# A mixture of experts behind two normalizations: rounds reordered, epsilons on GpSimd, rows on ScalarE, and experts of the slots found by partition

## The reference, cut to what matters

```python
h = (x - mu) * rsqrt(var + 1e-05) * ln_g + ln_b          # over the features of a token
h_norm = (h - m_t) * rsqrt(v_t + 1e-08)                  # over the tokens of a sequence, by feature
gamma, beta = ...                                        # a small network over the sequence's subject
h = h_norm * (softplus(gamma) + 1e-08) + beta
probs = softmax(h @ router_w)                            # 8 experts
gates, idx = top_k(probs, 2)                             # normalized to a sum of 1
y = sum over the two of gate * (relu(h @ w1[e] + b1[e]) @ w2[e] + b2[e])
x = x + y
...                                                      # gradients of x on a grid, one explicit step, max with 0
```

## Time and profile before

| what | value |
|---|---|
| median of 3 runs | 361.11 us (361.04 to 361.63) |
| profiled execution | 361.7 us, its span 359.9 us |
| TensorE busy | 306.2 us (85%) |
| VectorE busy | 291.9 us (81%) |
| ScalarE busy | 251.2 us (70%) |
| GpSimd busy | 156.8 us (44%) |
| rounds and routing | up to 72.9 us of the span |

### The profile page before, as it was taken

One profiled execution on the slowest core, in us unless ns is written; L12 is line 12 of the kernel. 1 busy time (PEld: TensorE's weight loads), 2 busy tenths in 40 slices (PEclk: granted clock), 3 DMA queues, 4 the chain that ended last, 5 costly groups with the idle time before them and its releaser, 6 DMA issues.

```text
span 359.9 us, 6561 instructions
## 1 busy us (share of the span) xinstructions
PE 306.2 (85%) x1961; PEld 265.4 (74%) x1961; DVE 291.9 (81%) x540; ACT 251.2 (70%) x462; POOL 156.8 (44%) x122
## 2 busy tenths in 40 slices
PE   1758312899999999999999999999999988379896
PEld 1548211889999999999999999999999978133334
DVE  4998892778899889988988989888898893289991
ACT  1668104596998799699789969969987870278421
POOL 1344424133335545533534554453354413277650
PEclk9999755799999999999999999999999999769999
DMA  7912508985688877866868786686784500595822
GB/s 248 387 35 73 162 1 291 358 270 207 220 263 264 292 241 224 272 226 215 283 231 274 263 277 195 240 258 214 227 277 157 157 4 29 158 308 111 184 96 82
DMA packets 49860, 74.46 MB, mean 207 GB/s; under 512 B 3349, under 2 KB 40623, under 8 KB 49712
## 3 DMA queue, kind: packets, MB, share of 16 engines
q1 hardware_dynamic: 45104, 62.29, 52.8%
q0 software_dynamic: 4368, 11.54, 10.6%
q10 hardware_dynamic: 368, 0.39, 0.4%
HBM read 63.69 MB, written 9.31 MB: 203 GB/s over the span
## 4 chain that ended last, share of the span: by engine, by line
PE 66%; DVE 15%; DMA 8%; issue 5%; POOL 2%; ACT 1%; SPq 1%; DVEq 0%; POOLq 0%; ACTq 0%
PE psum L991 23%; PE psum L1018 19%; PE psum L1020 10%; PE psum L984 5%; PE psum L960 2%; DMA x_sb<-in_x_dram 2%; PE psum L986 2%; DMA t_y<-y_rows 2%; PE psum L1013 2%; DMA raw_b<-in_L_cond_exp_w_dram 2%; DVE st L1149 1%; PE psum L1055 1%; DMA x_sb<-t_y 1%; DVE z L1139 1%; DVE h_tok L1175 1%
## 5 line engine op out<-in xcount | busy, mean ns | idle before, releaser
L787 POOL DMA_INDIRECT gathered<-h_rows,src_cur x40 | 62.1, 1554 | 119.6 <-DVE src_cur L1321 105.7
L1018 PE MATMUL psum<-w_split,hid 128*128 128x512 f32 x296 | 107.2, 404 | 1.5 <-DVE y_sb L1373 1.5
L991 PE MATMUL psum<-slot_h,w_split 128*128 128x256 f32 x768 | 96.5, 286 | 2.5 <-DVE slot_h L1338 2.5
L991 PEld LDWEIGHTS psum<-slot_h,w_split 128*128 128x128 f32 x768 | 94.6, 193 | 3.6 <-issue 3.0
L1020 PE MATMUL psum<-w_split,hid 128*128 128x256 f32 x296 | 83.1, 281 | 0.0
L1332 DVE TENSOR_TENSOR w_split<-raw_b,w_split 128x2048 fp32r<-128x2048 f32 x23 | 52.7, 2292 | 22.3 <-ACT w_split L605 22.3
L1018 PEld LDWEIGHTS psum<-w_split,hid 128*128 128x128 f32 x296 | 55.6, 188 | 14.4 <-issue 1.7
L637 ACT ACTIVATE hid<-relu 128x512 fp32r<-128x512 f32 (+1 forms) x92 | 51.1, 592 | 16.0 <-DVE relu L1344 16.0
L800 POOL DMA_INDIRECT y_rows<-y_sb,dst_cur x39 | 48.7, 1249 | 28.8 <-issue 11.6
L628 ACT ACTIVATE relu<-psum,b_cur 128x256 f32<-128x256 f32 x128 | 53.7, 490 | 6.2 <-PE psum L991 4.1
L1326 DVE TENSOR_TENSOR w_split<-raw_a,w_split 128x2048 fp32r<-128x2048 f32 x23 | 52.6, 2286 | 6.0 <-DMA gathered<-h_rows,src_cur 5.0
(11 more groups left out here) (181 smaller groups left out, 403.9 us busy)
## 6 DMA issues: line engine op xcount, KB each, us to landing
raw_a<-in_L_cond_exp_w_dram SPq DMA_DIRECT2D x23, 1024.0 KB, 6.0
raw_b<-in_L_cond_exp_w_dram SPq DMA_DIRECT2D x23, 1024.0 KB, 5.7
t_y<-y_rows SPq DMA_DIRECT2D x6, 512.0 KB, 8.7
x_sb<-in_x_dram SPq DMA_DIRECT2D x4, 512.0 KB, 7.9
h_rows<-h_tok SPq DMA_DIRECT2D x16, 128.0 KB, 2.2
x_sb<-t_y POOLq DMA_DIRECT2D x4, 512.0 KB, 4.7
out_dram<-t_out SPq DMA_DIRECT2D x3, 512.0 KB, 3.0
b_all<-in_L_cond_exp_b_dram SPq DMA_DIRECT2D x1, 1024.0 KB, 10.9
```

Source lines behind the costliest of these rows:

```text
L787: pool.indirect_dma_start(out=gathered[:, par, t, :], out_offset=None, in_=h_rows, in_offset=bass.IndirectOffsetOnAxis(ap=src_cur[:, par, ...
L991: last = pe.matmul(banks[bank][:, ST * (blk % 2):ST * (blk % 2) + rows], w_split[:, 0, par, w, at:at + P], slot_h[:, par, h, k, 0:rows], s ...
L1018: pe.matmul(out.rearrange("p (w d) -> p w d", w=2), hid[:, par, 0, blk, P * t:P * t + P], w_split[:, 1, par, :, D * blk:D * blk + D], star ...
```

## The change

- The two additions of epsilon (`var1`, `var2`) move from VectorE to GpSimd, ahead of each power.
- A round on VectorE is written in another order: both kinds of statistics, then `z`, then (rounds 9 to 11) the copy `rows` of sequences 1 to 3, then `aff_a`, the aggregations, `aff_m` and `aff_b`. Semaphores of their own replace `link`.
- ScalarE makes the copies `rows` of sequences 0, 6 and 7; VectorE keeps 1 to 5.
- TensorE runs `forward(6)` ahead of `back(0)`, and `back(1)` behind `forward(7)`.
- The experts of the slots are found with a slot on each of 23 partitions, on VectorE: two comparisons and a sum over the experts. TensorE turns the column of 23 into a row, and VectorE copies it to `e_idx` behind `pick`. GpSimd's three operations go, and 366 columns of constants with them. `gathered_part` is only padding that keeps the addresses.
- `low_w1(0)` waits for `first_sent`, which GpSimd raises behind the two gathers of slot 0, and not for their landing.

Declarations of semaphores are left out of the diff.

```diff
@@ -88,8 +88,8 @@
     c[:, C_BEFORE:C_BEFORE + P] = p[:, None] < p[None, :]
     c[:, C_LATER:C_LATER + NJ * E] = np.tile(np.arange(E) > 0, NJ)
     lead = np.array([first_col(s) for s in range(NS)])
-    c[:, C_SLOT:C_SLOT + NS * E] = np.repeat(lead // TB, E)
-    c[:, C_SLOT + NS * E:C_SLOT + 2 * NS * E] = np.repeat(np.where(lead < ROWS, E, NC - 1 - lead), E)
+    c[0:NS, C_SLOT] = lead // TB
+    c[0:NS, C_SLOT + 1] = np.where(lead < ROWS, E, NC - 1 - lead)
     c[:, C_PART] = p
     c[:, C_PART + 1] = p + 1
     d1, d2 = stencil(T)
@@ -263,8 +263,9 @@
             row_of = own("row_of", [P, P, TOPK * NJ], F16)
             col_of = own("col_of", [P, NC, TOPK * NJ], F16)
             token_of = own("token_of", [P, TOPK * NJ], F16)
-            e_cmp = own("e_cmp", [1, 2, NS, E])
-            e_sum = own("e_sum", [1, NS])
+            e_cmp = own("e_cmp", [NS, 2, E])
+            e_sum = own("e_sum", [NS, 1])
+            own("gathered_part", [P, 2 * NS * E + NS - 2 * E - 1])
             second = own("second", [P, NC])
             empty = own("empty", [P, NC])
             token = own("token", [P, NC])
@@ -397,10 +401,11 @@
         STYLE = 5
         CHUNK = 8
         HELD = 6
+        BY_SCALAR = (0, NB - 2, NB - 1)
 
         def rows_taken(b):
 
-            return (htok_ok, b + 1)
+            return (htok_act, BY_SCALAR.index(b) + 1) if b in BY_SCALAR else (htok_ok, b)
 
         def rows_bank(b):
             return (6, 2, 0)[b % 3]
@@ -562,6 +567,13 @@
                                           bias=aff_b[:, b, k:k + 1], scale=aff_a[:, b, k:k + 1])
                 last.then_inc(ht_ok, 1)
 
+            def rows(b):
+
+                at = rows_bank(b)
+                act.wait_ge(back_t, b + 1)
+                act.activation(h_tok[:, 2 * b:2 * b + 2, 0:KD * P + E], psum[:, at:at + 2, 0:KD * P + E],
+                               ACT.Copy).then_inc(htok_act, 1)
+
             act.wait_ge(sty_in, 32)
             front(0)
             for n in range(STYLE - 1):
@@ -583,9 +595,13 @@
             styled(1)
             front(6)
             styled(2)
+            rows(0)
             front(7)
             for b in range(3, NB):
                 styled(b)
+
+            for b in BY_SCALAR[1:]:
+                rows(b)
 
             act.wait_ge(gap_ok, 1)
             act.activation(e2[:, :], gap[:, :], ACT.Exp).then_inc(e2_ok, 1)
@@ -754,10 +770,16 @@
             for i in range(NB + 3):
                 if i < NB:
                     pool.wait_ge(var1_ok, i + 1)
+                    pool.tensor_scalar(var1[:, 2 * i:2 * i + 2], mv1[:, 2 * i:2 * i + 2, 1], 1e-5, None,
+                                       ALU.add).then_inc(eps1_ok, 1)
+                    pool.wait_ge(eps1_ok, i + 1)
                     pool.tensor_tensor(rs1[:, 2 * i:2 * i + 2], var1[:, 2 * i:2 * i + 2], half[:, 0:2],
                                        ALU.pow).then_inc(rs1_ok, 1)
                 if i >= 3:
                     pool.wait_ge(var2_ok, i - 2)
+                    pool.tensor_scalar(var2[:, i - 3, :], mv2[:, i - 3, :, 1], 1e-8, None,
+                                       ALU.add).then_inc(eps2_ok, 1)
+                    pool.wait_ge(eps2_ok, i - 2)
                     pool.tensor_tensor(rs2[:, i - 3, :], var2[:, i - 3, :], half[:, 0:KD],
                                        ALU.pow).then_inc(rs2_ok, 1)
             for c in range(TOPK):
@@ -765,17 +787,6 @@
                 number(token_of[:, NJ * c:NJ * c + NJ], [[sign * P, NJ]], base=sign, by_partition=sign)
             number(col_of[:, :, :], [[1, NC], [0, TOPK * NJ]])
             number(row_of[:, :, :], [[1, P], [0, TOPK * NJ]])
-
-            pool.wait_ge(off_ok, 1)
-            pool.tensor_tensor(e_cmp[:, :, :, :],
-                               cst[0:1, C_SLOT:C_SLOT + 2 * NS * E].rearrange("p (c s e) -> p c s e", c=2, e=E),
-                               t_off[0:1, :, :].rearrange("p c (a e) -> p c a e", a=1).broadcast_to([1, 2, NS, E]),
-                               ALU.subtract).then_inc(e_link, 1)
-            pool.wait_ge(e_link, 1)
-            flags = e_cmp[:, :, :, :].rearrange("p c s e -> p (c s e)")
-            pool.tensor_scalar(flags, flags, 0.0, None, ALU.is_ge).then_inc(e_link, 1)
-            pool.wait_ge(e_link, 2)
-            pool.tensor_tensor(e_cmp[:, 0, :, :], e_cmp[:, 0, :, :], e_cmp[:, 1, :, :], ALU.mult).then_inc(e_link, 1)
 
             def gather(k, m):
                 s, par = at_slot(k, m), k % 2
@@ -805,6 +816,8 @@
             pool.wait_ge(hrows_out, 16 * (NJ + 1))
             for k in range(FIRST):
                 gather(k, None)
+                if k == 0:
+                    pool.sem_inc(first_sent, 1)
             for k in range(2, FIRST):
                 gather(k + 2, None)
                 scatter(k - 2, None)
@@ -922,12 +935,11 @@
             forward(3)
             forward(4)
             forward(5)
+            forward(6)
             pe.wait_ge(eye_ok, 1)
             back(0)
-            forward(6)
-            back(1)
             forward(7)
-            for b in range(2, NB):
+            for b in range(1, NB):
                 back(b)
 
             pe.wait_ge(m_ok, 1)
@@ -939,6 +951,8 @@
                                  m_bf[:, 0:NJ + 1 - d, :].rearrange("p j e -> p (j e)"), start=False, stop=(d == NJ))
             last.then_inc(rank_ok, 1)
 
+            pe.wait_ge(e_sum_ok, 1)
+            pe.matmul(banks[4][0:1, 0:NS], e_sum[:, :], ident[0:NS, 0:NS], start=True, stop=True).then_inc(e_turned, 1)
 
             pe.wait_ge(tok_ok, 1)
             for t in range(TOPK * NJ):
@@ -1130,6 +1144,12 @@
                         dve.wait_ge(x_in[i // 2], 16)
                     for j in range(2 * i, 2 * i + 2):
                         last = dve.bn_stats(st1[:, j, :], x_sb[:, j, :])
+                if do_chan:
+                    dve.wait_ge(pre_ok, chan + 1)
+                    for k in range(KD):
+                        last = dve.bn_stats(st2[:, chan, k, :], h_pre[:, k, T * chan:T * chan + T])
+                if do_tok or do_chan:
+                    chained(last)
                 b = i - 1
                 if tokens and 0 <= b < NB:
                     dve.wait_ge(rs1_ok, b + 1)
@@ -1139,32 +1159,26 @@
                         norm = dve.tensor_scalar(z[:, j % 4, :], x_sb[:, j, :], mv1[:, j, 0:1], rs1[:, j:j + 1],
                                                  ALU.subtract, ALU.mult)
                     norm.then_inc(z_ok, 1)
+                if i - NB in range(1, NB):
+                    rows(i - NB)
                 if do_aff:
                     dve.wait_ge(rs2_ok, b1)
-                    last = dve.tensor_tensor(aff_a[:, b0:b1, :], rs2[:, b0:b1, :],
-                                             gam[:, :, b0:b1].rearrange("p k b -> p b k"), ALU.mult)
-                if do_chan:
-                    dve.wait_ge(pre_ok, chan + 1)
-                    for k in range(KD):
-                        last = dve.bn_stats(st2[:, chan, k, :], h_pre[:, k, T * chan:T * chan + T])
-                if not (do_tok or do_aff or do_chan):
-                    return
-                link(last)
+                    dve.tensor_tensor(aff_a[:, b0:b1, :], rs2[:, b0:b1, :],
+                                      gam[:, :, b0:b1].rearrange("p k b -> p b k"), ALU.mult).then_inc(aff_a_ok, b1 - b0)
+                dve.wait_ge(chain, steps[0])
                 if do_tok:
                     for j in range(2 * i, 2 * i + 2):
                         last = dve.bn_aggr(mv1[:, j, :], st1[:, j, :])
-                if do_aff:
-                    last = dve.tensor_tensor(aff_m[:, b0:b1, :], mv2[:, b0:b1, :, 0], aff_a[:, b0:b1, :], ALU.mult)
+                    last.then_inc(var1_ok, 1)
                 if do_chan:
                     for k in range(KD):
                         last = dve.bn_aggr(mv2[:, chan, k, :], st2[:, chan, k, :])
-                link(last)
-                if do_tok:
-                    dve.tensor_scalar(var1[:, 2 * i:2 * i + 2], mv1[:, 2 * i:2 * i + 2, 1], 1e-5, None,
-                                      ALU.add).then_inc(var1_ok, 1)
-                if do_chan:
-                    dve.tensor_scalar(var2[:, chan, :], mv2[:, chan, :, 1], 1e-8, None, ALU.add).then_inc(var2_ok, 1)
+                    last.then_inc(var2_ok, 1)
                 if do_aff:
+                    dve.wait_ge(aff_a_ok, b1)
+                    dve.tensor_tensor(aff_m[:, b0:b1, :], mv2[:, b0:b1, :, 0], aff_a[:, b0:b1, :],
+                                      ALU.mult).then_inc(aff_m_ok, b1 - b0)
+                    dve.wait_ge(aff_m_ok, b1)
                     dve.tensor_tensor(aff_b[:, b0:b1, :], sty[:, KD:2 * KD, b0:b1].rearrange("p k b -> p b k"),
                                       aff_m[:, b0:b1, :], ALU.subtract).then_inc(aff_ok, b1 - b0)
 
@@ -1172,8 +1186,8 @@
 
                 dve.wait_ge(back_t, b + 1)
                 at = rows_bank(b)
```

(23 more changed lines are left out.)

11 lines of the change are left out of this document (7 added, 4 removed).

## The result

The changed kernel took 358.56 us (median of 5 runs, 356.84 to 359.56), the kernel before 361.04 on the same chip (360.43 to 361.63): a ratio of 0.9922, 95% interval 0.9897 to 0.9948. The profiled execution took 359.56 us with a span of 357.7.

What follows compares the result with a forecast made beforehand. The chain ending last was taken to bound it: normalization rounds, routing, first gather, w2 load, then matmuls. 0.55 + 1.14 - 1.05 = 0.64 won gave 361.06 profiled, 360.5 as median; range 358.7 to 361.8 us.

Steps and rivals of the forecast that it cites:

- the rounds: Normalization rounds up to the first maximum mx: mx at 38.4 instead of 38.95, 0.55 us won.
- the stretch behind the first gather: W2 load (5.68 us), its split, then matmuls from 72.90: taken as unchanged, passing earlier gains on in full.
- Routing, 1.14 forecast: Finding the experts, from t_off on: 1.14 us won, or 0.2 if the slow VectorE instructions have another cause.
- First gather, 1.05 lost: Slot 0's second gather meets the early w1 subtraction and lands at 62.55 instead of 61.5: 1.05 us lost.
- the equal gaps of 0.30: Equal 0.30 us gaps between gather starts, read as GpSimd's sequencer running ahead, so first_sent rises before the second gather.
- The rival in which the gather isn't met: first_sent rises late or w1 is split after 58.2; the gather wins 0.5, time 358.9; chance 0.29.
- The rise of TensorE's rate: Doubling of TensorE's pass rate, placed near 30.0 during back(1); front 1.0 won if at 29, 0.3 if at 32.
- e: Price of one epsilon addition on GpSimd, taken as 0.40 us, between a memset (0.11) and a power (0.69).
- The rival of a better front: e near 0.16 or TensorE's rate doubled by 29: front wins 1.1, time 359.9 with the gather met; chance 0.12.
- From there on the chain is matmuls behind matmuls: From 72.90, the slots' matmuls: an earlier microsecond won counts in full at the end.
- swallowed by round 4: Smaller constants may bring x_sb sooner, but round 4's wait for h_pre of sequence 1 takes that gain up.
- Dear epsilons, the slower rival: Additions on GpSimd cost 1.16 us like its only tensor_scalar, rounds become GpSimd's, time 367; chance 0.14.

Runs made afterwards that it cites:

- the parts alone: Two kernels, each the kernel before with one half of the change: the new rounds, 359.23 us; the new way to find the experts, 358.60 us.
- the landing awaited: The changed kernel with low_w1(0) waiting again for the landing of slot 0's gather: 357.13 us, ratio 0.9890.
- epsilons twice: The changed kernel with each epsilon added on GpSimd as two halves, one behind the other: 360.07 us (one run).
- the nine and the six matmuls: Unread matmuls behind forward(5), low_w1(0) awaiting the landing: nine, 357.13 us; six, with the copies rows(1) to rows(3) behind the affine factors, 355.79 us.

## Why the prediction was wrong, point by point

Two steps failed: the rounds, whose term of 0.55 measured 1.57, and the stretch behind the first gather, taken over unchanged, where the w2 load took 0.56 more and the slots 0.75 less. The routing and the first gather came out as summed.

**Routing, 1.14 forecast: right.** 1.11 in the result, 1.12 between the parts alone. `base` fell from 0.85 to 0.15 when GpSimd's operations went, as the prediction read it; an instruction of VectorE was also put ahead of it, so that cause isn't shown by itself. TensorE's turn of the 23 values, put at some 0.6 from no row, took 0.23 and was hidden.

**First gather, 1.05 lost: right in mechanism and nearly in size, incomplete in reach.** The gather was met, as the equal gaps of 0.30 had it; 0.94 lost to the landing. The step that failed is the load behind it, taken over at 5.68: the w2 load took 6.24, since it started among the rows of slot 1's gathers, whose generation ended 0.68 us past its issue (60.44 against 59.76). In the kernel before it ended 0.13 past it:

```profile
60.69 0.94 POOL L787 DMA_INDIRECT gathered<-h_rows,src_cur  x1 [0.30 <-issue]
```

Together 1.5. The load of w1 for slot 2 isn't the cause, though it goes out sooner: 1.79 us into the w2 load here, 2.56 before, but 2.57 again with the landing awaited, where the w2 load still takes 6.13. The rival in which the gather isn't met was given 0.5 won by a faster landing. With the landing awaited that gain is there (2.75 for 3.32) and the w2 load takes it back (6.13 for 5.68).

**Rounds, 0.55 forecast: the term that failed, by its size.** The order of events was right to the names. The rise of TensorE's rate, placed near 30.0 from one trace, came at 30.0 in the profiled execution; that was luck, since it came at 27.0 with the same program in another, worth 1.35 of `mx`. So at the forecast's own place of the rise the term measured 1.57, 1.02 more than forecast. Of that 0.68 was won when `rows(1)` started, at 29.82 instead of 30.5, since z of sequence 6 stood at 23.42 instead of 24.2; the other 0.34 lies between `rows(1)` and `mx`, 7.56 where 7.9 was summed. What was mis-sized is above all e: it was 0.22, not the 0.40 midway between a memset and a power. By "epsilons twice", where 0.30 of e moves z by 0.98, the 0.18 too much make some 0.6 at z (an estimate), and they count once more, 0.18, in the last addition ahead of `mx`. The other quarter of a microsecond is the rest of the sum, priced a little long. How steeply `mx` depends on e was right: by the prediction's figures for 0.10, 0.40 and 0.69 an e of 0.52 costs 0.8 more than one of 0.22, and at an equal rise it cost some 0.9. The rival of a better front (doubling by 29, or e near 0.16) came nearest, at 1.1.

**"From there on the chain is matmuls behind matmuls", counted in full: not so.** The matmuls of the slots themselves became 0.75 faster, because narrower constants moved the tiles. The prediction read the 366 columns as a shorter load alone, and that part (swallowed by round 4) was right.

**Dear epsilons, the slower rival: fell.** The trace's only `tensor_scalar`, 1.16 on 368 elements, was no guide to two elements. The Trainium skill, GPSIMD Engine Reference, section Engine selection, wants elementwise work on VectorE, but puts its price on operations of two inputs and calls those of one input roughly line-rate, and the addition of an epsilon has one. The traces here have the addition at 0.22 to 0.26 us on GpSimd and 0.15 to 0.17 on VectorE, and moving it back to VectorE won nothing.

In the terms of the sum: 0.55 + 1.14 - 1.05 = 0.64 became 1.57 + 1.11 - 0.94 - 0.56 + 0.75 = 1.93, and 0.22 in the tail. The tail varied from 49.3 to 50.5 between executions, so that 0.22 can't be put down to the change. That the medians differ by 2.48 and the profiled executions by 2.14 lies within what the rise of TensorE's rate alone moves.

**Open.** What makes TensorE's rate rise 3.0 us apart in two executions whose work up to it agrees within 0.05 isn't settled; earlier work moves it, as the nine and the six matmuls show, with the two earliest rises of all (25.2 and 23.0). The Trainium skill, TensorE: Matmul & The Clock Gate, Part 1, says that the chip's look at TensorE's activity runs freely and isn't set to a program's start; that would fit, and no run here shows it. The same part of the Trainium skill lets the moment vary by half a microsecond either way; the 3.0 us measured here go beyond that.

## What to carry to other kernels

A copy out of PSUM that waits for TensorE holds up all that stands behind it on VectorE: write the short factors that the next engine needs ahead of it. A semaphore raised behind a gather in GpSimd's list isn't a sign that the gather runs; whoever starts a long subtraction upon it runs into that gather. And a change of a constant's width moves every tile behind it: before a small gain is put down to the instructions, the long loop should be compared on its own. And before the fronts of two executions are compared, see from their passes where TensorE's rate rises in each.

## What the hardware showed unexpectedly

- A `tensor_scalar` on 128x2 takes 0.22 to 0.26 us on GpSimd, about a third of the power of the same elements (0.71), and VectorE's takes 0.15 to 0.17.
- TensorE's passes go from 6 to 11 a microsecond at moments 3.0 us apart in two executions of one program, with the granted clock at 1.00 throughout.
- 240 matmuls of 512 columns average 402 ns or 405 ns by where their tiles lie, 1,464 bytes apart: with the rest of the loop, 0.7 to 0.9 us from the seventh scatter to the last.
- A load of w2 took 5.4 us with slot 1's gathers held back until it was under way, 5.7 before, where their generation ended 0.1 us past its issue, and 5.9 to 6.3 in the eleven executions where it ended 0.7 us past it.
- An indirect gather that starts inside a 128x2048 subtraction of VectorE lasts 2.31 to 2.48 us and ends some 0.85 us behind it; clear of it the same gather takes 0.97 to 0.99.
